# Attention scores on the TensorE array: whole array with zero-padded keys, or two halves of 64 rows

## The chip, the cores and the metric

The kernel runs on one core of a Trainium2 chip. The metric is device time in microseconds (us) of one execution.

## The reference

Cross-attention for x of 8 batches x 1024 queries x 640 features and a context of 64 tokens x 1024 features for each batch. Of the 64 tokens 56 are text and 8 are image tokens with a mask made from boxes. There are 20 heads of 32 features.

```
q = heads(x @ w_q)
k, v       = heads(text @ w_k), heads(text @ w_v)            # 56 keys
k_ip, v_ip = heads(ip @ w_k_ip), heads(ip @ w_v_ip)          # 8 keys
out = softmax(q k^T / sqrt(32)) v  +  softmax(q k_ip^T / sqrt(32) + mask) v_ip
out = merge_heads(out) @ w_out + b_out + x
```

Everything is float32. The kernel keeps its precision by splitting each operand of a product into a high part, rounded to float32r, and a low part, the rest; a product is the sum of three matmuls, high x high, high x low, low x high (`three`, L103).

## The kernel before

**Data layout.** x, q and the output have features on the 128 partitions, in KD = 5 tiles of 128 features, that is four heads each (HPT = 4). Queries go in groups of GQ = 512, two groups a batch, NG = 16 groups in all; a group has GT = 4 query tiles of 128.

**Setup (to about 92 us).** Weights are loaded and split; keys and values of the context are computed for all batches and go through k_scratch and v_scratch in HBM; the first q is computed.

**Keys.** k_raw holds the keys of one batch, a tile m of four heads by KEYS = 64 keys. A score matmul contracts over all 128 features of a tile, four heads at once, so the keys are laid out in blocks: k_hi and k_lo are [128, 5, 4, 64], and head j's keys stand only in its own 32 partitions and its own block j (`k_head`, L138); all else is zero, set once by two memsets (L279). The moving operand of one score matmul is one m of it, 4 x 64 = 256 columns, of which each row of the array has 64 that aren't zero. ScalarE writes the high parts (`k_hi_part`, four activations a batch), VectorE the low ones (`k_lo_part`).

**Scores.** The stationary operand is qT_hi or qT_lo, 128 features x 128 queries. `score_unit` (L841) fills one PSUM bank of 512 columns with two (query tile t, feature tile m) blocks of 256 scores, three matmuls each; a group has UNITS = 10 such units, on banks 0 to 3 in turn. ScalarE copies each bank to prob (`copy_scores`, L649) in SBUF, where a query tile has 20 heads x 64 keys = 1280 columns. From the fifth unit on, TensorE waits for the copy of the unit four before.

**The order of a group** is written out by hand for each engine; engines meet at semaphores alone. TensorE (`group`, L896): 10 score units; the 5 output tiles of the group before (75 matmuls of 512 columns); the first 2 of the 5 q tiles of the next group (30 of 75); then transposes of the probabilities by pairs of heads (`p_transpose`, L859), the products with v (`pv_pair`, L873) and the remaining 45 q matmuls interleaved. ScalarE: the score copies, with oT_hi of the group before after the second; exponentials; residual; copies of transposed probabilities and of results. GpSimd: adding the mask to the last 8 keys of each head when the tile's copies are done (`add_mask`, which waits for `units_for_tile`), in the order tiles 0, 1, 2, then subtracting the maximum from the tiles, the mask of tile 3 after tile 0, and then multiplying by the inverse sums (`normalise`). VectorE: maxima, sums, inverses, low parts, adding.

The transposes of a group can start only when GpSimd's `normalise` is done. Between the scores and the transposes TensorE has the output tiles and the q tiles.

Of the kernel before, what the change touches and what calls it, by code (L numbers as in the profile page):

```python
# [27 lines left out]
P = 128  # L28
# [11 lines left out]
def attention_kernel(nc, xT_dram, textT, ipT, bbox, w_q, w_k, w_v, w_k_ip, w_v_ip, w_out, b_out, grid_x, grid_y, outT):  # L40
# [14 lines left out]
    UNITS = GT * SW // 512  # L55
    HALF = D // 2
# [10 lines left out]
    with whole:  # L67
# [16 lines left out]
        k_hi, k_lo = sb("k_hi", [P, KD, HPT, KEYS], F32R), sb("k_lo", [P, KD, HPT, KEYS], F32R)  # L84
# [53 lines left out]
        def k_head(t, j):  # L138
            return t[j * DH:(j + 1) * DH, :, j, :]

        def k_hi_part(act, b):
            act.wait_ge(k_raw_loaded, 16 * (b + 1))
            for j in range(HPT):
                nc.scalar.activation(k_head(k_hi, j), k_raw[j * DH:(j + 1) * DH, :, :], ACT.Copy).then_inc(k_hi_built, 1)

        def k_lo_part(dve, b):
            for j in range(HPT):
                dve.wait_ge(k_hi_built, HPT * b + j + 1)
                nc.vector.tensor_tensor(k_head(k_lo, j), k_raw[j * DH:(j + 1) * DH, :, :], k_head(k_hi, j).bitcast(F32), ALU.subtract).then_inc(k_built, 1)
# [6 lines left out]
        with setup:  # L156
# [73 lines left out]
            with nc.Block() as block:  # L230
# [42 lines left out]
                @block.gpsimd  # L273
                def _(pool):
                    nc.gpsimd.memset(ident[:], 0.0).then_inc(ident_zeroed, 1)
                    pool.wait_ge(ident_zeroed, 1)
                    nc.gpsimd.affine_select(out=ident[:], in_=ident[:], compare_op=ALU.not_equal, fill=1.0, base=0,
                                            pattern=[[-1, P]], channel_multiplier=1).then_inc(ident_made, 1)
                    for buf in (k_hi, k_lo):  # L279
                        nc.gpsimd.memset(buf[:].rearrange("p m j k -> p (m j k)").bitcast(F32), 0.0).then_inc(k_zeroed, 1)  # L280
                    for c in range(1, len(chunks), 2):
                        hi, lo = split_dst(c)
                        pool.wait_ge(w_hi_done, c + 1)
                        nc.gpsimd.tensor_tensor(lo, w_raw[:, c % LOADS, :], hi.bitcast(F32), ALU.subtract).then_inc(w_lo_done[1], 1)

                @block.scalar
                def _(act):
# [42 lines left out]
                    for m in range(KD):  # L330
# [3 lines left out]
                        if m == KD - 3:  # L334
                            act.wait_ge(k_zeroed, 2)
                            k_hi_part(act, 0)
# [173 lines left out]
        def units_for_tile(t):  # L510

            return -(-(t + 1) * SW // 512)

        def tile(t):
            return prob[:, t * SW:(t + 1) * SW].rearrange("p (h k) -> p h k", k=KEYS)

# [43 lines left out]
        with nc.Block() as block:  # L560
# [87 lines left out]
            def _(act):  # L648
                def copy_scores(g, u):  # L649
                    act.wait_ge(score_ready, UNITS * g + u + 1)  # L650
                    nc.scalar.activation(prob[:, u * 512:(u + 1) * 512], s_bank[u % 4][:], ACT.Copy).then_inc(score_copied, 1)  # L651
# [188 lines left out]
            def _(pe):  # L840
                def score_unit(g, n, b, new_batch):  # L841
                    if n < 2:
                        wait(pe, score_copied, UNITS * g)
                    elif n < 4:
                        wait(pe, pT_lo_done, PAIRS * g)
                    else:
                        pe.wait_ge(score_copied, UNITS * g + n - 3)
                    if n == 0 and new_batch:
                        pe.wait_ge(k_built, HPT * (b + 1))
                    for half in range(2):  # L850
                        t, m = divmod(2 * n + half, KD)
                        if t == 0:
                            pe.wait_ge(q_lo_done, KD * g + m + 1)
                        q_cols = slice(t * P, (t + 1) * P)
                        keys = [k[:, m, :, :].rearrange("p j k -> p (j k)") for k in (k_hi, k_lo)]
                        ins = three(s_bank[n % 4][:, half * CW:(half + 1) * CW], qT_hi[:, m, q_cols], qT_lo[:, m, q_cols], *keys, True, True)
                    ins.then_inc(score_ready, 1)
# [38 lines left out]
                def group(g, b, new_batch, before, more, shared=0):  # L896
                    for n in range(UNITS):
                        score_unit(g, n, b, new_batch)
# [69 lines left out]
```

## Time and profile before

| | us |
|---|---|
| median of 2 runs | 929.83 (929.28 to 930.37) |
| span of the profiled execution | 927.5 |
| median less that span | 2.3 |
| TensorE matmul busy | 894.0 (96%) |
| VectorE busy | 732.2 (79%) |
| ScalarE busy | 605.7 (65%) |
| GpSimd busy | 520.5 (56%) |

The profile is of one execution. Its span goes from the first to the last instruction; the time of the run that was profiled isn't given beside it, so it is compared with the median. Recorded matmuls overlap, as each lasts until its results are written: how dense they are is told by the distance between starts. "PEld" rows are the loads of the stationary operand that each matmul brings with it. In the rows, "k_hi,qT_hi" means moving and stationary operand of a matmul; the three kinds of a product stand under the lines L104, L105 and L106 of `three`, whoever calls it. float32r operands are shown as f32.

### The profile page before, as it was taken

The page shows a single profiled execution, that of the slowest core. Times are in us where ns is not written, and L with a number is a line of the kernel's source. Part 1 is how long each engine was busy: PE and PEld are TensorE (multiplying, and loading weights), DVE is VectorE, ACT ScalarE, POOL GpSimd, SP SyncE. Part 2 cuts the span into 40 slices and gives each one's busy share as a digit, 9 for nine tenths or more (in the row PEclk, how much of TensorE's full clock was granted, in tenths as well). Part 3 has the DMA queues.
Part 4 walks back from the last instruction along what each step waited for, and adds up shares of the span by engine and source line. Part 5 has one row for each costly group of instructions (what it writes and reads, how often), then busy time and mean ns, then how long its engine had stood idle before and what let it go on. Part 6 is the DMA issues. An engine that isn't in the chain of part 4 may idle for free.

```text
span 927.5 us, 13827 instructions
## 1 busy us (share of the span) xinstructions
PE 894.0 (96%) x4685; PEld 749.3 (81%) x4685; DVE 732.2 (79%) x999; ACT 605.7 (65%) x982; POOL 520.5 (56%) x422
## 2 busy tenths in 40 slices
PE   7999869999999999999999999999999999999978
PEld 7977748888878788888888788888888887888856
DVE  6484888888787969787887879787887879697872
ACT  5464767585848577675858586775768485866751
POOL 3372638465573929374664839283755739292731
PEclk9999999999999999999999999999999999999989
DMA  8684020303030210303030301203030302010001
GB/s 264 222 275 162 22 71 1 121 1 128 1 121 1 72 55 4 116 0 127 0 120 0 121 6 38 83 0 127 0 120 0 127 0 91 22 47 12 35 23 57
DMA packets 34151, 64.79 MB, mean 70 GB/s; under 512 B 4428, under 2 KB 6604, under 8 KB 33996
## 3 DMA queue, kind: packets, MB, share of 16 engines
q1 hardware_dynamic: 32812, 61.82, 20.2%
q10 hardware_dynamic: 1312, 2.62, 0.9%
q8 instruction: 16, 0.26, 0.1%
q14 instruction: 11, 0.09, 0.0%
HBM read 40.84 MB, written 23.59 MB: 69 GB/s over the span
## 4 chain that ended last, share of the span: by engine, by line
PE 58%; DVE 18%; POOL 6%; issue 5%; ACT 2%; DVEq 0%; POOLq 0%
PE bank L104 15%; PE bank L106 14%; PE bank L105 14%; PE bank L870 7%; DVE total L764 5%; DVE xT_lo L118 5%; PE bank L879 4%; PE bank L880 4%; POOL prob L551 3%; DVE res L773 3%; POOL prob L606 2%; ACT prob L651 1%; DVE o_raw L753 1%; DVE top L758 1%; DVE pT_lo L746 1%
## 5 line engine op out<-in xcount | busy, mean ns | idle before, releaser
L618 POOL TENSOR_TENSOR oT_lo<-o_raw,oT_hi 128x512 fp32r<-128x512 f32 x80 | 103.3, 1292 | 266.2 <-ACT oT_hi L671 266.2
L551 POOL TENSOR_TENSOR prob<-prob,top 128x1120 f32<-128x1120 f32 x124 | 174.4, 1435 | 0.0
L557 POOL TENSOR_TENSOR prob<-prob,inv 128x1120 f32<-128x1120 f32 x124 | 164.4, 1361 | 6.9 <-DVE inv L766 6.9
L104 PE MATMUL bank<-xT_hi,wq_hi 128*128 128x512 f32 x400 | 163.0, 408 | 2.6 <-DVE qT_lo L136 2.6
L104 PE MATMUL bank<-oT_hi,wo_hi 128*128 128x512 f32 x400 | 159.8, 400 | 3.1 <-DVE res L773 2.3
L105 PE MATMUL bank<-oT_lo,wo_hi 128*128 128x512 f32 x400 | 158.0, 395 | 0.0
L106 PE MATMUL bank<-oT_hi,wo_lo 128*128 128x512 f32 x400 | 157.9, 395 | 0.0
L106 PE MATMUL bank<-xT_hi,wq_lo 128*128 128x512 f32 x400 | 157.0, 393 | 0.0
L105 PE MATMUL bank<-xT_lo,wq_hi 128*128 128x512 f32 x400 | 155.9, 390 | 0.0
L753 DVE TENSOR_TENSOR o_raw<-bank,pv_part 64x512 f32<-64x512 f32 x160 | 110.2, 689 | 49.1 <-ACT pv_part L667 45.1
L758 DVE TENSOR_REDUCE top<-prob 128x20 f32<-128x1120 f32 (+1 forms) x128 | 98.7, 814 | 43.6 <-POOL prob L606 43.3
L658 ACT ACTIVATE prob<-prob 128x1280 f32<-128x1280 f32 x64 | 81.5, 1275 | 77.9 <-POOL prob L551 76.7
L667 ACT ACTIVATE pv_part<-bank 64x512 f32<-64x512 f32 x160 | 94.8, 593 | 40.3 <-PE bank L880 37.1
L132 ACT ACTIVATE qT_hi<-bank 128x512 fp32r<-128x512 f32 x80 | 47.3, 591 | 103.6 <-PE bank L106 101.0
L746 DVE TENSOR_TENSOR pT_lo<-bank,pT_hi 128x512 fp32r<-128x512 f32 x160 | 108.0, 683 | 3.5 <-ACT pT_hi L662 1.5
L662 ACT ACTIVATE pT_hi<-bank 128x512 fp32r<-128x512 f32 x160 | 94.1, 599 | 12.8 <-PE bank L870 9.7
L118 DVE TENSOR_TENSOR xT_lo<-xin,xT_hi 128x512 fp32r<-128x512 f32 x80 | 101.2, 1282 | 0.0
L651 ACT ACTIVATE prob<-bank 128x512 f32<-128x512 f32 x160 | 92.6, 598 | 11.3
L870 PEld LDWEIGHTS bank<-ident,prob 128*128 128x128 f32 x640 | 79.8, 142 | 23.2 <-POOL prob L557 3.6
L870 PE MATMUL bank<-ident,prob 128*128 128x128 f32 x640 | 95.1, 275 | 3.1 <-POOL prob L557 3.1
L764 DVE TENSOR_REDUCE total<-prob 128x20 f32<-128x1120 f32 (+1 forms) x128 | 98.0, 805 | 0.0
L104 PEld LDWEIGHTS bank<-oT_hi,wo_hi 128*128 128x128 f32 x400 | 75.0, 188 | 27.0 <-DVE res L773 9.0
(88 smaller groups left out, 1754.3 us busy)
## 6 DMA issues: line engine op xcount, KB each, us to landing
outT<-res SPq DMA_DIRECT2D x80, 256.0 KB, 6.7
xin<-in_xT SPq DMA_DIRECT2D x14, 1280.0 KB, 6.7
w_raw<-in_L_xattn_w_v SPq DMA_DIRECT2D x8, 320.0 KB, 5.3
w_raw<-in_L_xattn_w_k SPq DMA_DIRECT2D x8, 320.0 KB, 3.6
w_raw<-in_L_xattn_w_v_ip SPq DMA_DIRECT2D x8, 320.0 KB, 3.8
w_raw<-in_L_xattn_w_k_ip SPq DMA_DIRECT2D x8, 320.0 KB, 3.7
xin<-in_xT ACTq DMA_DIRECT2D x2, 1280.0 KB, 8.0
v_raw<-v_scratch SPq DMA_DIRECT2D x16, 160.0 KB, 4.2
```

The costliest lines, as they stand in the source:

```text
L104: nc.tensor.matmul(dst, a_hi, b_hi, start=first, stop=False)
L105: nc.tensor.matmul(dst, a_hi, b_lo, start=False, stop=False)
L106: return nc.tensor.matmul(dst, a_lo, b_hi, start=False, stop=last)
L118: nc.vector.tensor_tensor(x_tile(xT_lo, k), xin[:, u, k, :], x_tile(xT_hi, k).bitcast(F32), ALU.subtract).then_inc(xT_lo_done, 1)
L551: ins = eng.tensor_tensor(s, s, top[:, t, n, :].unsqueeze(2).broadcast_to([P, HEADS, k1 - k0]), ALU.subtract)
L557: ins = eng.tensor_tensor(s, s, inv[:, t, n, :].unsqueeze(2).broadcast_to([P, HEADS, k1 - k0]), ALU.mult)
L618: nc.gpsimd.tensor_tensor(oT_lo[:, m, :], o_raw[:, m % 2, :], oT_hi[:, m, :].bitcast(F32), ALU.subtract).then_inc(oT_lo_done, 1)
L746: nc.vector.tensor_tensor(pT_lo[:, p % 2, :], t_bank[p % 2][:], pT_hi[:, p % 2, :].bitcast(F32), ALU.subtract).then_inc(pT_lo_done, 1)
L753: nc.vector.tensor_tensor(o_raw[own, m % 2, :], v_bank[p % 2][own, :], pv_part[own, :], ALU.add).then_inc(pv_added, 1)
L758: ins = nc.vector.tensor_reduce(top[:, t, n, :], tile(t)[:, :, k0:k1], AX.X, ALU.max)
L764: nc.vector.tensor_reduce(total[:, t, span, :], tile(t)[:, :, k0:k1], AX.X, ALU.add).then_inc(sum_done, 1)
L870: ins = nc.tensor.transpose(t_bank[p % 2][:, t * P:(t + 1) * P], src, ident[:])
```

## The change

The array is used in two halves of 64 rows, r = 0 and r = 1. Each half contracts over two heads, 64 features, and its moving operand has only these two heads' keys: PW = 2 x 64 = 128 columns. The results of the two halves are different columns of the scores, and they go to different banks: a pair of banks (n, n + 1) is filled by RUN = 4 steps (t, m); bank n gets the first two heads of the four steps, bank n + 1 the others. So each step has 3 x 2 matmuls of 64 rows and 128 columns, the halves in turn. Both banks of a pair are ready after the last step, and TensorE waits before each pair for both banks. The copies on ScalarE write four runs of 128 columns. The zero-padded keys are one buffer, k_parts, with high and low parts and two head blocks for each. units_for_tile gives 4, 6, 8, 10 where it gave 3, 5, 8, 10.

```diff
+    PW = 2 * KEYS
+    RUN = 512 // PW
...
-        k_hi, k_lo = sb("k_hi", [P, KD, HPT, KEYS], F32R), sb("k_lo", [P, KD, HPT, KEYS], F32R)
+        k_parts = sb("k_parts", [P, KD, 2, 2, KEYS], F32R)
...
-        def k_head(t, j):
-            return t[j * DH:(j + 1) * DH, :, j, :]
+        def k_head(part, j):
+            return k_parts[j * DH:(j + 1) * DH, :, part, j % 2, :]
...
-                    for buf in (k_hi, k_lo):
-                        nc.gpsimd.memset(buf[:].rearrange("p m j k -> p (m j k)").bitcast(F32), 0.0).then_inc(k_zeroed, 1)
+                    nc.gpsimd.memset(k_parts[:].rearrange("p m s j k -> p (m s j k)").bitcast(F32), 0.0).then_inc(k_zeroed, 1)
...
         def units_for_tile(t):
-            return -(-(t + 1) * SW // 512)
+            return 2 * -(-(t + 1) * KD // RUN)
...
+        def score_dst(u):
+            blocks = prob[:, u // 2 * RUN * CW:(u // 2 + 1) * RUN * CW].rearrange("p (n r c) -> p r n c", r=2, c=PW)
+            return blocks[:, u % 2, :, :]
...
-                    nc.scalar.activation(prob[:, u * 512:(u + 1) * 512], s_bank[u % 4][:], ACT.Copy).then_inc(score_copied, 1)
+                    nc.scalar.activation(score_dst(u), s_bank[u % 4][:].rearrange("p (n c) -> p n c", n=RUN), ACT.Copy).then_inc(score_copied, 1)
...
-                def score_unit(g, n, b, new_batch):
-                    if n < 2:
+                def score_units(g, u, b, new_batch):
+                    n = 2 * u
+                    if u == 0:
                         wait(pe, score_copied, UNITS * g)
-                    elif n < 4:
+                    elif u == 1:
                         wait(pe, pT_lo_done, PAIRS * g)
                     else:
-                        pe.wait_ge(score_copied, UNITS * g + n - 3)
-                    if n == 0 and new_batch:
+                        pe.wait_ge(score_copied, UNITS * g + n - 2)
+                    if u == 0 and new_batch:
                         pe.wait_ge(k_built, HPT * (b + 1))
-                    for half in range(2):
-                        t, m = divmod(2 * n + half, KD)
+                    for i in range(RUN):
+                        t, m = divmod(RUN * u + i, KD)
                         if t == 0:
                             pe.wait_ge(q_lo_done, KD * g + m + 1)
-                        q_cols = slice(t * P, (t + 1) * P)
-                        keys = [k[:, m, :, :].rearrange("p j k -> p (j k)") for k in (k_hi, k_lo)]
-                        ins = three(s_bank[n % 4][:, half * CW:(half + 1) * CW], qT_hi[:, m, q_cols], qT_lo[:, m, q_cols], *keys, True, True)
-                    ins.then_inc(score_ready, 1)
+                        q_cols, dst = slice(t * P, (t + 1) * P), slice(i * PW, (i + 1) * PW)
+                        for q_part, k_part in ((qT_hi, 0), (qT_hi, 1), (qT_lo, 0)):
+                            for r in range(2):
+                                rows = slice(r * HP, (r + 1) * HP)
+                                ins = nc.tensor.matmul(s_bank[(n + r) % 4][:, dst], q_part[rows, m, q_cols], k_parts[rows, m, k_part, :, :].rearrange("p j k -> p (j k)"),
+                                                       start=q_part is qT_hi and k_part == 0, stop=q_part is qT_lo)
+                                if i == RUN - 1 and q_part is qT_lo:
+                                    ins.then_inc(score_ready, 1)
```

## Rows read from the trace of the kernel before

**Rows 1.** The page: busy us, share and instructions; granted TensorE clock in tenths, 40 slices.

```profile
PE 894.0 (96%) x4685; PEld 749.3 (81%) x4685; DVE 732.2 (79%) x999; ACT 605.7 (65%) x982; POOL 520.5 (56%) x422
...
PEclk9999999999999999999999999999999999999989
```

**Rows 2.** The waits of TensorE: us in total, times, longest us.

```profile
PE bank L879 <- DVE pT_lo L746: 11.3, 17, 2.0
PE bank L104 <- DVE ipT_parts L380: 6.0, 1, 6.0
PE bank L870 <- POOL prob L557: 3.1, 2, 2.6
PE bank L104 <- DVE qT_lo L136: 2.6, 1, 2.6
...
PE bank L104 <- DVE res L773: 2.3, 13, 0.2
```

**Rows 3.** Windows: a score stage and a whole group; us, then busy us (instructions), clock.

```profile
499.45:506.75 7.30, 7.30 (x61) 7.30 (x61) 4.98 (x7) 6.69 (x12) 3.33 (x5) 1.00 0.00 0
...
499.45:550.90 51.45, 51.27 (x271) 43.08 (x271) 42.04 (x58) 34.85 (x57) 30.53 (x26) 1.00 0.17 57
```

**Rows 4.** Groups by line and shape: count, busy us, mean ns, idle before.

```profile
L104 PE MATMUL bank<-k_hi,qT_hi 128*128 128x256 f32 x320 | 91.2, 285 | 1.6 <-PEq L230 1.1 <-ACT prob L651 0.5
...
L651 ACT ACTIVATE prob<-bank 128x512 f32<-128x512 f32 x160 | 92.6, 598 | 11.3
```

**Rows 5.** Timeline of TensorE, start and end of that score stage: start us, us.

```profile
499.47 0.37 PE L104 MATMUL bank<-k_hi,qT_hi 128*128 128x256 f32 x1
499.68 0.28 PE L105 MATMUL bank<-k_lo,qT_hi 128*128 128x256 f32 x1
499.80 0.28 PE L106 MATMUL bank<-k_hi,qT_lo 128*128 128x256 f32 x1
...
499.45 0.19 PEld L104 LDWEIGHTS bank<-k_hi,qT_hi 128*128 128x128 f32 x1 [0.26 <-issue]
499.56 0.19 PEld L105 LDWEIGHTS bank<-k_lo,qT_hi 128*128 128x128 f32 x1
499.68 0.19 PEld L106 LDWEIGHTS bank<-k_hi,qT_lo 128*128 128x128 f32 x1
499.80 0.19 PEld L104 LDWEIGHTS bank<-k_hi,qT_hi 128*128 128x128 f32 x1
...
506.63 0.28 PE L106 MATMUL bank<-k_hi,qT_lo 128*128 128x256 f32 x1
506.75 0.40 PE L104 MATMUL bank<-oT_hi,wo_hi 128*128 128x512 f32 x1
...
506.63 0.19 PEld L104 LDWEIGHTS bank<-oT_hi,wo_hi 128*128 128x128 f32 x1
```

**Rows 6.** Timeline of TensorE in the setup, matmuls of 320 columns, first and last of six.

```profile
12.80 0.31 PE L104 MATMUL bank<-qT_hi,ctxT_hi 128*112 128x320 f32 x1
...
13.53 0.31 PE L106 MATMUL bank<-qT_hi,ctxT_lo 128*112 128x320 f32 x1
```

**Rows 7.** Weight loads by shape, windows 14 to 30 and 40 to 60 us: mean ns.

```profile
L106 PEld LDWEIGHTS bank<-qT_hi,ctxT_lo 128*112 128x112 f32 x37 | 6.5, 174 | 0.0
...
L104 PEld LDWEIGHTS bank<-ctxT_hi,qT_hi 128*128 128x128 f32 x21 | 3.9, 187 | 3.8 <-POOL qT_lo L284 3.5
```

**Rows 8.** Timeline and source line: the five transposes of k_ip; min/median/max ns.

```profile
74.02 0.39 PEld L468 LDWEIGHTS bank<-ident,k_ip 64*128 64x128 f32 x5 [0.31 <-issue]
...
L468 PEld LDWEIGHTS bank<-ident,k_ip x5: 134/140/140, 74.0 to 74.3; 64*128 64x128 f32 x5
```

**Rows 9.** Timeline of TensorE: the next group's first eight transposes and what follows.

```profile
531.53 1.03 PE L870 MATMUL bank<-ident,prob 128*128 128x128 f32 x8
532.32 0.48 PE L104 MATMUL bank<-xT_hi,wq_hi 128*128 128x512 f32 x1
```

**Rows 10.** Timeline of ScalarE over that score stage.

```profile
499.36 1.21 ACT L667 ACTIVATE pv_part<-bank 64x512 f32<-64x512 f32 x2
500.59 1.20 ACT L651 ACTIVATE prob<-bank 128x512 f32<-128x512 f32 x2
501.69 0.62 ACT L671 ACTIVATE oT_hi<-o_raw 128x512 fp32r<-128x512 f32 x1
502.21 5.34 ACT L651 ACTIVATE prob<-bank 128x512 f32<-128x512 f32 x8
```

**Rows 11.** Timeline of GpSimd: the last normalisations of that group.

```profile
518.88 10.54 POOL L557 TENSOR_TENSOR prob<-prob,inv 128x1120 f32<-128x1120 f32 x8
```

**Rows 12.** Source line of the key memsets: min/median/max ns, first and last start us.

```profile
L280 POOL MEMSET k_hi<- x1: 1164/1164/1164, 1.4 to 1.4; 128x1280 f32 x1
L280 POOL MEMSET k_lo<- x1: 1164/1164/1164, 2.5 to 2.5; 128x1280 f32 x1
```

More of the change, by code:

```diff
@@ L143, in k_hi_part @@
             for j in range(HPT):
-                nc.scalar.activation(k_head(k_hi, j), k_raw[j * DH:(j + 1) * DH, :, :], ACT.Copy).then_inc(k_hi_built, 1)
+                nc.scalar.activation(k_head(0, j), k_raw[j * DH:(j + 1) * DH, :, :], ACT.Copy).then_inc(k_hi_built, 1)
         def k_lo_part(dve, b):
@@ L148, in k_lo_part @@
                 dve.wait_ge(k_hi_built, HPT * b + j + 1)
-                nc.vector.tensor_tensor(k_head(k_lo, j), k_raw[j * DH:(j + 1) * DH, :, :], k_head(k_hi, j).bitcast(F32), ALU.subtract).then_inc(k_built, 1)
+                nc.vector.tensor_tensor(k_head(1, j), k_raw[j * DH:(j + 1) * DH, :, :], k_head(0, j).bitcast(F32), ALU.subtract).then_inc(k_built, 1)
         def load_k(sp, b):
@@ L334, in _ @@
                         if m == KD - 3:
-                            act.wait_ge(k_zeroed, 2)
+                            act.wait_ge(k_zeroed, 1)
                             k_hi_part(act, 0)
@@ L896, in group @@
                 def group(g, b, new_batch, before, more, shared=0):
-                    for n in range(UNITS):
-                        score_unit(g, n, b, new_batch)
+                    for u in range(UNITS // 2):
+                        score_units(g, u, b, new_batch)
                     if before:
```

## The prediction

> **What bounds the kernel now.** I read the page's busy times first. TensorE has 894.0 of 927.5 us, its clock was granted at nine or ten tenths throughout, and no other engine passes 80% [rows 1]. Busy matmul time can deceive, so next the waits of TensorE: the largest sum is 11.3 us, behind VectorE's pT_lo, and all the others together come to some 19 us [rows 2]. Then one whole group of 512 queries in the windows: 51.45 us, of which TensorE records 51.27 as busy [rows 3]. Sixteen such groups run one after another, 823 of the 927.5 us. So in the steady state the end is set by how closely TensorE's instructions follow each other, and what a score stage costs TensorE, the whole kernel pays sixteen times. The stage itself lasts 7.30 us and holds 60 matmuls of 256 columns; recorded durations (283 ns) overlap, and it is the spacing that counts [rows 3, 4, 5].
>
> **What a score matmul costs now.** In the timeline each starts 0.12 us after the one before, and the load of the next weights starts at the very moment the current matmul starts [rows 5]. Is the matmul or the load the limit? At 320 columns six starts lie 0.146 us apart [rows 6]. At 2.4 GHz, one column each cycle, 320 columns take 133 ns and 256 take 107: both leave 13 ns. So the streaming is the limit and the load is hidden, but only just. Where a load is not hidden, at the first score matmul after a pause, the second load follows 0.11 us after the first [rows 5]. The shape table supports this price: loads of 112 columns are recorded at 174 ns, loads of 128 at 187 or 188, so 16 columns are worth 14 ns, and 128 of them 110 [rows 7]. These are rows of 128 partitions; a load of the float32r kind with 64 partitions is nowhere in the trace.
>
> The Trainium skill, "TensorE: Matmul & The Clock Gate", section "LDWEIGHTS (loading the stationary operand)", gives columns / 1.2 ns, 107 ns for 128 columns, whatever the number of rows; the rows above agree with its size, and that 64 rows cost the same is shown by none.
>
> **The change, part by part.**
>
> Columns. The zeros of the other two heads of a tile are no longer streamed: a (tile, m, part) step moves 128 columns in each half and not 256 in the whole array. If both halves stream at once, this is 53 + 13 = 66 ns for a step instead of 120.
>
> Instructions and loads. 60 matmuls become 120, and each still brings its own load of 128 weight columns: 120 loads instead of 60. Removed: streaming. Doubled: everything paid per instruction. Three prices for a pair of halves follow. (a) Streaming alone, 66 ns. (b) The load of the next pair can't hide behind 53 ns of streaming: 110 to 120 ns if the two halves load side by side, 220 to 240 if one after the other. (c) The closest spacing of two matmuls anywhere in the trace is that of the five small transposes of k_ip, 64 rows and 64 columns: their five loads span 0.39 us, the last of them 0.14, so 0.0625 us apart [rows 8]. If that is the pace of issue, a pair can't take less than 125 ns. The transposes of 128 columns are no tighter than 0.11 us each (eight from 531.53 to about 532.4) [rows 9]. I take 125 ns: the halves use different rows, different partitions of SBUF and different banks, and it is the price from the row that is nearest in size, with 64 rows. The ends for the range are 66 and 240. So 60 pairs take 7.5 us, and with the 0.10 us of the exposed first load 7.6, against 7.30 now: **+0.3 us a group**.
>
> Score copies. They stay 160 ScalarE copies of 128x512, 598 ns each [rows 4]; the destination becomes four runs of 128 elements, for which I count nothing; a run of 128 floats is long, and if it did cost 50 ns each, 10 copies would be 0.5 us a group, of which the next point shows about half on the path. But two banks now come ready together, after 24 matmuls (1.5 us) and not after 6 (0.7 us). ScalarE today is free 1.12 us after the stage begins (pv_part ends at 500.57), copies from 500.59, has oT_hi after the second copy, and ends the ten at 507.55 [rows 10]. After the change it starts at about +1.75 us. The pair of banks for the fourth step is free when 4 copies are done: 1.75 + 2.4 + 0.42 for oT_hi = 4.6, plus some 0.1 of signalling, against 4.6 us at which TensorE would be there: **+0.1 to 0.25 us**, take 0.2. For the fifth step 6 copies are needed, at 5.8, and TensorE arrives at 6.3: no wait. Behind a waiting TensorE is only its own stream; ScalarE, on the other hand, ends its copies 0.6 us later.
>
> Leaving the halves. Today the first wo_hi load is issued at 506.63, during the last score matmul, and hidden [rows 5]. After it the array goes back from half to full rows. If that load must wait for the halves, 0.11 us are exposed, and with the end of the last matmul (283 less 120 ns) up to 0.28. Entering is less: the stage already begins with an exposed load. I take **+0.15 us**.
>
> The Trainium skill, "TensorEngine Tiling (Array Packing)", section "Key Properties", says that changing the tiling mode drains TensorE; by it the upper end of 0.28 us would hold at both ends of the stage, and the sum would be some 6 us longer. No row here has such a change of mode.
>
> Masks and probabilities. GpSimd's mask for tile 0 now waits for 4 copies, not 3, and for tile 1 for 6, not 5; for tiles 2 and 3 for 8 and 10 as before. GpSimd's long chain (subtract, normalise) starts in order behind the mask of tile 2, so with copy 8, some 0.5 us later. It ends at 529.42 today, the transposes that need it start at 531.53 [rows 9, 11]: 2.1 us of slack, and they move later themselves. Nothing is added. If this slack were gone, a delay of the copies would be paid in full, 0.6 x 16 = 10 us.
>
> Key buffers. k_hi and k_lo (2 x 1280 words a partition) become k_parts with half of that; one memset of 1.16 us in place of two at 1.4 us into the kernel [rows 12], used 85 us later: nothing. The splits into high and low parts have the same 32x320 shapes, same strides in kind: nothing. No DMA is changed.
>
> **The sum.** 0.3 + 0.2 + 0.15 = 0.65 to 0.7 us a group, 16 groups: +11 us on the span of 927.5, so 938.5; the median of the runs (929.83) stands 2.3 us above that span: **941 us**.
>
> **Rivals.**
>
> 1. *The two halves load one after the other.* Place: each of the 120 loads; price: 0.11 us each, 13.2 and 0.1 us for the stage against 7.3, +6.0 and 0.15 for leaving, x 16 = +98: **1028 us** (1023 to 1047 for 107 to 120 ns). It decides as soon as a pair needs more than about 137 ns (8.3 us for the stage, +19 us, 2%). For it: today every load begins only when the matmul before it has begun, as if one could be ahead at a time [rows 5], and if that order is kept across the halves, 64 rows buy nothing. Against it: that same timing is explained as well by the one spare set of weights, which is free only when the matmul starts, and the halves have each their own. The k_ip loads (64 rows, 0.0625 us apart) prove only that small float32 loads are short. 30%.
> 2. *The halves overlap in part*: loads side by side, but one matmul streams after the other with something lost in each turn, or every bank change stalls: 150 to 200 ns a pair, 9.1 to 12.1 us for the stage, +31 to +79: **961 to 1009 us**. Nothing speaks for one value. 10%.
> 3. *The pair really takes the time of its streaming*, 66 ns, because a load of 64 rows is short and the pace of issue isn't 62 ns. Then ScalarE's copies set the stage: six copies and oT_hi must be done before the last step, 1.14 + 6 x 0.6 + 0.43 + 0.1 = 5.3 us, and 0.8 for it: 6.1 against 7.3, less 0.15 for leaving, so -1.0 x 16: **914 us**, just inside 2%. Against it: 110 ns for a load of this kind in two readings [rows 5, 7]. 8%.
>
> The Trainium skill, "TensorEngine Tiling (Array Packing)", sections "Theoretical Speedup" and "PSUM Bottleneck", promises up to 2x for a contraction of at most 64 rows and warns that the emptying of PSUM may then be the bottleneck; that is this third case.
>
> That the change doesn't do what it says (both halves stream in turn, loads hidden) would be 2 x 66 = 132 ns a pair, +0.7 us a group instead of +0.3: 947 us, and lies in the forecast's own range.
>
> **How the numbers follow.** Forecast 941 with its neighbours (pairs of 110 to 135 ns, leaving 0 to 0.3 us), 926 to 952: 52%. With the rivals at 30, 10 and 8% that is everything. Two per cent, about what a measurement of this kernel can tell from no change, is 911.2 to 948.4. Faster: the better half of rival 3, 3%. Within: 48% of the forecast's 52, nearly 5% of rival 3, 2% of the rest: 55%. Slower: 42%. The range reaches from 914 up to 1034, leaving out 4% below and the upper third of rival 1 and stray cases above.
>
> **What will show it.** In the timeline of the score stage, the starts of two neighbouring matmuls of different halves and of two of the same half: 0.12 to 0.13 us for the latter and a stage of about 8 us if I am right, 0.21 to 0.24 and a stage near 13 us under rival 1, under 0.1 us and a stage near 6 under rival 3. The load rows: whether two loads of different halves start together. A wait of TensorE for a score copy before the fourth step of a group, and none for it under rival 1. The first wo_hi load: during the last score matmul, or after it. The prediction is wrong if the halves load in turn, and above all if ScalarE's copies with their four runs are longer than 0.65 us.

## The result: 943.35 us, 1.5% slower, and the profile after

The changed kernel takes **943.35 us** (median of two runs, 938.98 and 947.71) against 929.83 before; the ratio is 1.0148 [1.0123, 1.0172]. Run again beside other kernels it took 939.75 us, ratio 1.0102 [1.0085, 1.0119]. Its profiled execution spans 937.2 us, 9.7 more than the one before. That is the forecast's size (941). But of its terms one has the wrong sign, one that was put at nothing is as large as the whole loss of a group, and one was not in it.

The page of the changed kernel: busy times; the granted clock of TensorE in 40 slices; two groups of instructions.

```profile
PE 899.8 (96%) x5645; PEld 749.1 (80%) x5645; DVE 723.4 (77%) x999; ACT 599.4 (64%) x982; POOL 518.1 (55%) x421
...
PEclk9999799999999999999999999999999999999999
...
L865 PE MATMUL bank<-k_parts,qT_hi 64*128 64x128 f32 x1280 | 114.9, 281 | 1.9 <-PEq L232 1.0
...
L657 ACT ACTIVATE prob<-bank 128x512 f32<-128x512 f32 x160 | 86.8, 597 | 26.2 <-PE bank L865 26.0
```

TensorE has 960 instructions more (60 x 16) and is busy for only 6 us more. The copies are as long as before, 597 ns against 598 [rows 4]; their idle time before them has grown from 11.3 to 26.2 us, nearly all of it spent waiting for score banks. The fifth slice of the clock is new.

The waits of TensorE in the changed kernel (us in total, times, longest).

```profile
PE bank L106 <- DVE res L779: 9.1, 15, 0.6
...
PE bank L865 <- ACT prob L657: 0.9, 1, 0.9
```

One row has moved: the wait for VectorE's res, 2.3 us in 13 waits [rows 2], is 9.1 in 15. That is the wait before an output tile. The wait for a score copy stands here once in the whole run, so what it costs in every group is read from starts, below.

Windows of the changed kernel: the ninth group's score stage and the whole group (us, then busy us and instructions of TensorE, its loads, VectorE, ScalarE, GpSimd; granted clock; DMA).

```profile
506.43:513.47 7.04, 7.04 (x121) 6.89 (x120) 3.83 (x6) 5.75 (x11) 2.77 (x4) 1.00 0.00 0
506.43:558.30 51.87, 51.24 (x333) 42.60 (x332) 41.62 (x58) 34.47 (x57) 30.64 (x26) 1.00 0.17 57
```

**The stage is shorter** by 0.26 us [rows 3], **and the group longer** by 0.42. Before, stages alternate between 7.28 and 7.20 us, groups between about 51.46 and 51.37, so the mean change is -0.20 and +0.45. In the table further down, the first two rows and 0.09 us of the leaving add up to the stage's change, all four rows to the group's.

The timeline of TensorE and of its loads, changed kernel, at the start and the end of that stage (start us, us). The timeline merges neighbours that are alike; the second row is what starts in the 10 ns from 506.43.

```profile
506.11 0.39 PE L891 MATMUL bank<-pT_lo,v_parts 128*128 128x512 f32 x1
506.43 0.33 PE L865 MATMUL bank<-k_parts,qT_hi 64*128 64x128 f32 x2
...
506.71 0.27 PE L865 MATMUL bank<-k_parts,qT_lo 64*128 64x128 f32 x2
506.82 0.39 PE L865 MATMUL bank<-k_parts,qT_hi 64*128 64x128 f32 x4
507.04 0.27 PE L865 MATMUL bank<-k_parts,qT_lo 64*128 64x128 f32 x2
...
513.27 0.27 PE L865 MATMUL bank<-k_parts,qT_lo 64*128 64x128 f32 x2
513.47 0.50 PE L106 MATMUL bank<-oT_hi,wo_hi 128*128 128x512 f32 x1
513.81 0.39 PE L107 MATMUL bank<-oT_lo,wo_hi 128*128 128x512 f32 x1
...
506.43 0.19 PEld L865 LDWEIGHTS bank<-k_parts,qT_hi 64*128 64x128 f32 x2 [0.35 <-issue]
...
513.47 0.19 PEld L106 LDWEIGHTS bank<-oT_hi,wo_hi 128*128 128x128 f32 x1
```

Both loads of a pair and both matmuls start within the same 10 ns. Three pairs (four matmuls on qT_hi, two on qT_lo) take 0.33 us, 506.71 to 507.04, so a pair takes 0.111. The prediction's sign for being right was a stage of about 8 us; this one, 7.04, is neither that nor the 13 or 6 of its rivals. The first wo_hi load now starts at 513.47, after the last score matmul and not with it [rows 5].

The timelines of ScalarE and GpSimd of the changed kernel: the copies, and the mask of tile 2.

```profile
506.25 1.21 ACT L673 ACTIVATE pv_part<-bank 64x512 f32<-64x512 f32 x2
508.02 1.09 ACT L657 ACTIVATE prob<-bank 128x512 f32<-128x512 f32 x2 [0.56 <-PE bank L865]
...
509.51 1.09 ACT L657 ACTIVATE prob<-bank 128x512 f32<-128x512 f32 x2
...
512.24 1.09 ACT L657 ACTIVATE prob<-bank 128x512 f32<-128x512 f32 x2 [0.40 <-PE bank L865]
...
513.51 0.52 POOL L612 TENSOR_TENSOR prob<-prob,mask 128x160 f32<-128x160 f32 x1 [0.47 <-ACT prob L657]
```

Copies come in twos, each two behind a pair of banks; the fourth two, from 512.24, end at 513.33, 6.90 us into the stage. Where that delay is paid is seen ten microseconds later. First the kernel before, then the changed one: TensorE before the fifth output tile, with the VectorE steps that release it and the mask of tile 2 at the head of their chain.

```profile
506.30 0.53 POOL L606 TENSOR_TENSOR prob<-prob,mask 128x160 f32<-128x160 f32 x1 [1.04 <-ACT prob L651]
...
518.52 1.53 DVE L764 TENSOR_REDUCE total<-prob 128x20 f32<-128x1120 f32 x2
520.41 0.63 DVE L773 TENSOR_TENSOR res<-bank,res 128x512 f32<-128x512 f32 x1
...
520.52 0.39 PE L106 MATMUL bank<-oT_hi,wo_lo 128*128 128x512 f32 x1
521.09 0.50 PE L104 MATMUL bank<-oT_hi,wo_hi 128*128 128x512 f32 x1 [0.18 <-DVE res L773]
```

```profile
525.80 1.53 DVE L770 TENSOR_REDUCE total<-prob 128x20 f32<-128x1120 f32 x2
527.69 0.63 DVE L779 TENSOR_TENSOR res<-bank,res 128x512 f32<-128x512 f32 x1
...
527.34 0.40 PE L108 MATMUL bank<-oT_hi,wo_lo 128*128 128x512 f32 x1
528.37 0.50 PE L106 MATMUL bank<-oT_hi,wo_hi 128*128 128x512 f32 x1 [0.63 <-DVE res L779]
```

Matmuls here are 0.23 us apart. Before, the fifth tile came 0.57 after its predecessor, now 1.03. The fifth tile needs a bank that VectorE's `output` of the third tile empties, and that addition stands in VectorE's order behind `sums` of query tile 1, which waits for the exponentials, which wait for GpSimd's subtraction, which stands behind the mask of tile 2, which waits for copy 8. From that mask's start to the late matmul it is 14.8 us before and 14.9 after: the chain was without slack already, and what delays copy 8 delays TensorE. The loss of 0.34 us was there before the change in nearly every group, and the last row of [rows 2], 13 waits, is where it stood.

### The profile page after: what moved, and what is told of

The parts are those of the page before. It is cut to its first block, busy times and chain, and to the rows that moved or that the text cites. A ratio compares the mean times of both kernels' runs of the same rounds, so it can differ in the third digit from the quotient of the medians.

```text
span 937.2 us, 15707 instructions
## 1 busy us (share of the span) xinstructions
PE 899.8 (96%) x5645; PEld 749.1 (80%) x5645; DVE 723.4 (77%) x999; ACT 599.4 (64%) x982; POOL 518.1 (55%) x421
## 4 chain that ended last, share of the span: by engine, by line
PE 59%; DVE 17%; issue 7%; POOL 4%; ACT 3%; DVEq 0%; POOLq 0%; ACTq 0%
PE bank L106 12%; PE bank L108 11%; PE bank L107 11%; PE bank L865 10%; PE bank L881 7%; DVE total L770 5%; DVE xT_lo L120 5%; PE bank L890 4%; PE bank L891 4%; DVE res L779 3%; POOL prob L557 2%; POOL prob L612 2%; ACT prob L657 1%; DVE o_raw L759 1%; DVE top L764 1%
## 5 line engine op out<-in xcount | busy, mean ns | idle before, releaser
L865 PE MATMUL bank<-k_parts,qT_hi 64*128 64x128 f32 x1280 | 114.9, 281 | 1.9 <-PEq L232 1.0
L865 PEld LDWEIGHTS bank<-k_parts,qT_hi 64*128 64x128 f32 x1280 | 100.0, 193 | 9.1 <-issue 6.9
L657 ACT ACTIVATE prob<-bank 128x512 f32<-128x512 f32 x160 | 86.8, 597 | 26.2 <-PE bank L865 26.0
```

The costliest lines, as they stand in the source:

```text
L657: nc.scalar.activation(score_dst(u), s_bank[u % 4][:].rearrange("p (n c) -> p n c", n=RUN), ACT.Copy).then_inc(score_copied, 1)
L865: ins = nc.tensor.matmul(s_bank[(n + r) % 4][:, dst], q_part[rows, m, q_cols], k_parts[rows, m, k_part, :, :].rearrange("p j k -> p (j k)" ...
```

## The experiments

Each kernel is the one before or the changed one with the edit shown. "Steady group" is a group's length, score stage to score stage, for the third to the fourteenth group: 51.37 to 51.54 us before, 51.84 to 51.92 in the changed kernel.

### The price of a load

**b_whole_128**: the kernel before with every score matmul cut in two of 128 columns, all 128 rows.

```diff
-                        keys = [k[:, m, :, :] ... for k in (k_hi, k_lo)]
-                        ins = three(s_bank[n % 4][:, half * CW:(half + 1) * CW], ...)
+                        for r in range(2):
+                            keys = [k[:, m, 2 * r:2 * r + 2, :] ... for k in (k_hi, k_lo)]
+                            c0 = half * CW + r * CW // 2
+                            ins = three(s_bank[n % 4][:, c0:c0 + CW // 2], ...)
```

> The kernel before, but each score matmul of 256 columns is cut into two of 128 columns, both over the whole array (128 rows), so 120 matmuls and 120 loads in place of 60, nothing side by side. Theory (a load of 128 float32r columns takes 0.111 us and is the price of a matmul too short to hide it, and only loads of different halves run together): 0.111 us a matmul, score stage 13.3 us, and some 5.7 us a group more in the total, about 1015 to 1025 us. Rival (the 0.111 us for a pair of matmuls is the pace of issue, 0.055 us for each): stage 6.7 to 7.2 us, time 926 to 935 us.

Measured: 1040.3 us, ratio 1.1181 [1.1116, 1.1246]. Timeline of TensorE in this kernel, start of a stage:

```profile
552.27 0.31 PE L104 MATMUL bank<-k_hi,qT_hi 128*128 128x128 f32 x1
552.42 0.27 PE L105 MATMUL bank<-k_lo,qT_hi 128*128 128x128 f32 x1
552.53 0.27 PE L106 MATMUL bank<-k_hi,qT_lo 128*128 128x128 f32 x1
552.64 0.28 PE L104 MATMUL bank<-k_hi,qT_hi 128*128 128x128 f32 x1
```

0.111 us a matmul, the stage 13.35 to 13.45 us. A matmul of the whole height now costs the 0.111 us that a pair of halves costs. The same 0.11 us lies between the first two loads of a stage when the matmuls have 256 columns [rows 5], so it is the load and not the matmul, and what the halves buy is that two loads go side by side. The time is above the expectation because the stage isn't all: the steady group is 58.2 to 58.3 us, and TensorE's wait for res is there too (10.0 us in 14 waits). The second of its two runs also had a lower mean clock, 0.984 against 0.995, and took 10 us longer.

The Trainium skill, "TensorE: Matmul & The Clock Gate", section "LDWEIGHTS (loading the stationary operand)", has columns / 1.2 ns whatever the number of rows, an estimate of 107 ns for 128 columns; the 0.111 us for 128 and for 64 rows agree.

**a_rows_apart**: the changed kernel, but within a pair of banks all twelve matmuls of one half before the twelve of the other.

```diff
-                    for i in range(RUN):
+                    for r, i in [(r, i) for r in range(2) for i in range(RUN)]:
...
-                            for r in range(2):
```

> The changed kernel with the same 120 matmuls of 64 rows and 128 columns, but in each pair of banks the 12 of the first half all come before the 12 of the second. Theory (loads of one half wait for each other, only the two halves load side by side): 0.111 us a matmul, stage about 13.3 us, 1015 to 1025 us. Rival (pace of issue, or a 64-row load that simply takes half the time): 0.055 us a matmul, stage as in the changed kernel, 7.1 us, 935 to 945 us.

Measured: 1077.44 us, ratio 1.158 [1.1524, 1.1636]. Timeline of TensorE at full clock, then the window of a later stage, in this kernel:

```profile
391.52 0.39 PE L865 MATMUL bank<-k_parts,qT_hi 64*128 64x128 f32 x2
391.75 0.27 PE L865 MATMUL bank<-k_parts,qT_lo 64*128 64x128 f32 x1
391.75 0.49 PE L865 MATMUL bank<-k_parts,qT_hi 64*128 64x128 f32 x4
...
270.00:285.80 15.80, 15.80 (x121) 15.66 (x121) 6.53 (x9) 6.79 (x12) 5.45 (x7) 0.61 0.01 2
```

Matmuls of one half alone follow each other at 0.111 us, the same as a pair (two on qT_hi, then one on qT_lo 0.23 us later). The halves run at once only where matmuls of both stand close together in the program. Two surprises. At 391.75 the first of the second half starts while three of the first half, written ahead of it, have yet to start. And the granted clock falls in every score stage, to half, 1.2 GHz, for a part of it (0.61 on average in this one; stages of 13.3 to 16.5 us), which no profile with alternating halves shows in the stage of any group but the first. So its 147 us hold, besides the halves in turn, an overlap that was not intended and a low clock, and are no clean price.

**a_rows_by_three**: the halves alternate by three matmuls and not by one.

```diff
-                        for q_part, k_part in (...):
-                            for r in range(2):
+                        for r in range(2):
+                            for q_part, k_part in (...):
```

> The changed kernel, but in each step the three matmuls of the first half come before the three of the second. It shows how far ahead of matmuls that still wait a load of the other half can be taken. If only past one matmul: two of six loads overlap with one of the other half, four load times a step, 0.44 us, stage 8.9 us, time about 965 us. If past three or more: 0.335 us a step as in the changed kernel, stage 7.1 us, 943 us. If past none: 0.67 us a step, stage 13.3 us, 1020 us.

Measured: 939.66 us, ratio 1.0099 [1.0078, 1.012], a stage of 7.05 us: the changed kernel's time. Its timeline at the start of a stage:

```profile
402.82 0.44 PE L865 MATMUL bank<-k_parts,qT_hi 64*128 64x128 f32 x4
403.10 0.28 PE L865 MATMUL bank<-k_parts,qT_lo 64*128 64x128 f32 x2
```

In the program the order is hi, hi, lo of one half and then of the other; in the trace all four on qT_hi start before either on qT_lo. A matmul of the other half goes past those written before it. With three of one half in a row the order costs nothing; with twelve it does.

### Where the group gets longer

**b_pair_ready**: the kernel before, whole rows and 256 columns, but two banks become ready together, at the end of each 12 matmuls. The loop over 10 units becomes one over 5 pairs; for such a pair:

```diff
-                        pe.wait_ge(score_copied, UNITS * g + n - 3)
+                        pe.wait_ge(score_copied, UNITS * g + n - 2)
...
+                    order = [(i, 0, part) for i in range(2) for part in range(3)] + [(i, 1, part) for part in range(3) for i in range(2)]
+                    for i, half, part in order:
```

> The kernel before with its 60 whole-array matmuls of 256 columns, but ordered so that two banks are finished 0.12 us apart, after 12 matmuls, and TensorE waits for both banks of a pair: one part of the change, its readiness in pairs, without the halves. Theory (what the change costs in the steady groups comes in by the eighth score copy, which starts GpSimd's chain, and is paid at TensorE's wait before the fifth output tile): score stage still 7.2 us, the copies some 0.2 to 0.35 us later, the stretch from the first output matmul to the first transpose longer by about as much (24.8 to 25.1 us), 51.65 to 51.85 us a group, 933 to 936 us, clock of the first group unchanged. Rival (the added 0.4 us a group is the price of going in and out of the halves): nothing changes, 930 us.

Measured: 936.39 us, ratio 1.0065 [1.0044, 1.0085]. Its TensorE and ScalarE, by timeline, and the wait row:

```profile
422.55 0.39 PE L106 MATMUL bank<-oT_hi,wo_lo 128*128 128x512 f32 x1
423.50 0.50 PE L104 MATMUL bank<-oT_hi,wo_hi 128*128 128x512 f32 x1 [0.56 <-DVE res L773]
...
511.26 1.09 ACT L651 ACTIVATE prob<-bank 128x512 f32<-128x512 f32 x2 [0.35 <-PE bank L858]
...
PE bank L104 <- DVE res L773: 8.1, 15, 0.6
```

No halves, the stage 7.2 to 7.29 us as before, and yet the steady group is 51.73 to 51.97, about what was expected: **handing banks over two at a time is enough for the longer wait at the fifth output tile**, and for nearly all of the steady loss.

**b_mask** and **a_mask**: an attempt to make slack elsewhere. GpSimd starts the chain with tile 0 before it adds the mask of tile 2, except in the first and the last group, and VectorE makes its first two xT_lo parts one tile earlier.

```diff
                     add_mask(g, 1)
-                    add_mask(g, 2)
+                    if shared:
+                        add_mask(g, 2)
                     for t, count in tiles:
                         sub_max(g, t, count)
                         if t == 0:
+                            if not shared:
+                                add_mask(g, 2)
                             add_mask(g, 3)
...
-                        if before and t == 2:
+                        if before and t == (2 if shared else 1):
                             split_x(0, 2)
```

> The kernel before, with GpSimd subtracting the maximum of tile 0 before it adds the masks of tiles 2 and 3 (not in the first and the last group), and VectorE's first two xT_lo parts after the maxima of tile 1 instead of tile 2. GpSimd's chain then starts behind the copy of unit 5 and not of unit 8. Theory: TensorE's wait of 0.45 us (with the exposed load) before the fifth output tile goes, 51.0 us a group, 13 or 14 groups: 923 to 926 us, ratio 0.993 to 0.996. Rival (the chain is held elsewhere, VectorE's order above all): no change or up to 1% slower, because the output of tile 0 comes later behind the maxima of tile 3.

> The changed kernel with the same reordering on GpSimd and VectorE. Theory (the steady loss of the change was that chain alone; halves as such cost nothing net): its wait of 0.9 us before the fifth output tile goes, 51.0 us a group as in the same reordering of the kernel before, total 926 to 931 us, with 2 to 4 us more than that one from the half clock in the first group. Rival (going in and out of the halves costs TensorE 0.4 us a group): 0.4 us a group more than the reordered kernel before, some 6 us, plus the first group: 932 to 936 us.

Measured: b_mask 946.13 us, 1.0192 [1.0167, 1.0217], and a_mask 958.52, 1.0322 [1.0291, 1.0352]. Both miss, theory and rival. The VectorE timeline of b_mask:

```profile
412.38 1.64 DVE L118 TENSOR_TENSOR xT_lo<-xin,xT_hi 128x512 fp32r<-128x512 f32 x2 [1.26 <-ACT xT_hi L114]
```

VectorE, in its fixed order, now stands 1.26 us for an xT_hi of ScalarE, and its output tiles come later: TensorE's wait for res is 17.5 us in 18 waits in b_mask and 21.8 in 29 in a_mask. The edit moved more than the chain, so it tells nothing about the chain's slack.

**b_output2**, **a_output2**: VectorE's order alone. The output addition of the third tile goes ahead of `sums` of query tile 1, of which it needs nothing.

```diff
+                        if before and n == 1:
+                            output(g - 1, 1 - u, n + 1)
                         sums(g, t, n)
...
-                        if before:
+                        if before and n != 1:
                             output(g - 1, 1 - u, n + 1)
```

> The kernel before, with VectorE adding output tile 2 of the group before (which frees the bank of the fifth output tile) ahead of the sums of tile 1 instead of after them; nothing else. Theory (TensorE's wait before the fifth output tile is for this one instruction, which stands behind sums that wait for GpSimd's chain): the wait of 0.45 us with its exposed load goes, 51.0 us a group, 14 groups: 923 to 925 us, ratio 0.993 to 0.995. Rival (the chain is late by as much further on, at the q tiles or at the transposes): 929 to 931 us.

> The changed kernel with the same move of output tile 2 on VectorE. Theory: its wait of 0.9 us goes; score stage with way in and out 0.1 us more than nothing, so about 51.0 us a group as in the same move in the kernel before, and 2 to 4 us for the half clock in the first group: 926 to 930 us, ratio 0.996 to 1.000; level or faster than the kernel before. Rival (the halves cost 0.4 us a group on TensorE itself): 51.4 us a group, 934 us.

Measured: the kernel before with it 925.71 us, ratio **0.9962 [0.9949, 0.9975]**, faster than both kernels. Its steady groups take 50.98 to 51.38 us, and the list of waits has res with 0.2 us in one. The changed kernel with it takes 935.94, ratio 1.0073 [1.0043, 1.0104], steady groups 51.45 to 51.53: the theory misses, the rival's numbers come out. Its TensorE and VectorE show why:

```profile
479.41 0.39 PE L108 MATMUL bank<-oT_hi,wo_lo 128*128 128x512 f32 x1
480.05 0.49 PE L106 MATMUL bank<-xT_hi,wq_hi 128*128 128x512 f32 x1 [0.24 <-DVE res L779]
...
477.40 1.53 DVE L770 TENSOR_REDUCE total<-prob 128x20 f32<-128x1120 f32 x2
479.29 0.63 DVE L779 TENSOR_TENSOR res<-bank,res 128x512 f32<-128x512 f32 x1
```

The fifth tile no longer waits, and the first q tile, one place on, waits 0.4 us for the fourth addition, which still stands behind the sums. So the rival's numbers came out for another reason than the one that it gave.

The kernel before with it isn't quite free of this either. In five of its twelve steady groups, those of 51.26 us and more, the first q tile comes 0.47 us after the matmul before it and not 0.23, again just behind the fourth addition (574.36 to 574.99), and leaves its load exposed:

```profile
574.65 0.39 PE L106 MATMUL bank<-oT_hi,wo_lo 128*128 128x512 f32 x1
575.12 0.49 PE L104 MATMUL bank<-xT_hi,wq_hi 128*128 128x512 f32 x1
```

The other seven take 50.98 to 51.11.

**a_output23**: the fourth addition is moved the same way (`n in (1, 2)` in place of `n == 1`).

> The changed kernel with VectorE adding output tiles 2 and 3 of the group before each ahead of the sums that they stood behind (tile 2 alone moved TensorE's wait to the first q matmul, where output tile 3 frees the bank). Theory (halves cost TensorE itself nothing net: 0.09 us more at the entry, 0.1 at the exit, 0.15 to 0.25 less in the stage; the rest is VectorE and GpSimd being late): that wait of 0.5 us goes, 50.9 to 51.1 us a group, as in the whole-array kernel with output tile 2 moved (51.05 to 51.3), and with the half clock of the first group 928 to 931 us. Rival (0.4 us a group is lost in the halves whatever is reordered): 51.4 to 51.5 us a group, 934 to 937 us.

Measured in 12 runs: 929.5 us, ratio 0.9994 [0.9983, 1.0004], no difference from the kernel before. Windows of a score stage and of a group, and the wait row, in this kernel:

```profile
500.45:507.50 7.05, 7.05 (x122) 6.90 (x121) 3.81 (x6) 5.73 (x11) 2.76 (x4) 1.00 0.00 0
500.45:551.44 50.99, 50.99 (x333) 42.68 (x332) 41.31 (x58) 34.45 (x57) 31.02 (x26) 1.00 0.17 58
...
PE bank L106 <- DVE res L779: 0.6, 1, 0.6
```

TensorE has no pause in the whole group. It is 0.88 us shorter than in the changed kernel: the 0.80 of the wait and 0.1 of the load that it left exposed. Where neither waits, halves and whole rows take the same time for a group within 0.1 us: 50.99 to 51.01 here, 50.98 to 51.11 in b_output2. Whole rows with both additions moved were not run, and the best time on record stays that of whole rows, 925.71 us. The profiled spans of the two, 927.9 and 925.9, differ by the first group (2.3 us longer here, see below), the setup (1.3) and the last group (1.7, not looked into), less 3.2 in the groups between.

### The first group, and the spread of runs

**a_again** is the changed kernel unedited. **m_g0_whole** has the first group's scores in whole rows from k_hi and k_lo, and halves of the same buffers from the second group on (`score_units` if g > 0, else `score_unit`).

> The changed kernel once more, for an interval on its ratio and a second profile of the clock. Theory: the steady groups are the same as in the first profile (51.86 us each, 0.41 more than before), and the score stage of the first group again runs partly at half clock, so that its 7.98 us become about 12; ratio 1.010 to 1.016. Rival: the fall of the clock in the first group was chance; then that stage lasts 7.8 to 8.2 us, the span is near 933.5 and the ratio near 1.006.

> The changed kernel's halves in all groups but the first; the first group's scores are made over the whole array as in the kernel before (keys in the layout of before, which holds the same 128 columns for each half). Theory (the half clock in the first score stage comes from the matmuls of 64 rows): that stage runs at full clock and lasts 7.9 to 8.0 us, the total is 2 to 4 us less than the changed kernel's, 936 to 937 us; the later groups stay at 51.87 us. Rival (the clock falls there by chance or for the pause before it, whatever the matmuls): the stage is 9.6 us or more as before, 940 us.

Measured: a_again 939.75 us, 1.0102 [1.0085, 1.0119], span 936.8, and m_g0_whole 936.51, 1.0092 [1.0062, 1.0123], span 934.4. Windows of the changed kernel and of m_g0_whole in the first group's score stage, which begins at 92.8 and 93.0 us:

```profile
98.00:105.00 7.00, 7.00 (x65) 6.88 (x66) 4.08 (x5) 2.31 (x5) 2.46 (x4) 0.50 0.00 0
```

```profile
98.00:105.00 7.00, 7.00 (x44) 6.32 (x44) 5.56 (x7) 4.90 (x8) 5.21 (x7) 1.00 0.00 0
```

In the changed kernel the clock is at 1.2 GHz for 13.7 us from 95.3 on, pairs are 0.21 us apart, and the stage takes 11.92 us; in whole rows in the same place it stays at 2.4 GHz and takes 7.98, as before the change. a_again has the low clock for 6.8 us and a stage of 9.65, less than the 12 that were expected. So it goes in every profile: the seven kernels with halves in the first group have 6.8 to 17.1 us of low clock that begin in this stage, the seven with whole rows have none there. The span of m_g0_whole is 2.8 us below that of the changed kernel; the ratios of a_again and m_g0_whole overlap, so in the timed runs the gain isn't proved.

Whole rows are not immune elsewhere. Every profile but that of the kernel before has a low stretch of 3.4 us that begins somewhere from 113 to 141 us. In b_output2 it falls into the score stage of the second group, which follows a stretch in which TensorE was busy for 2.35 of 3.9 us; that stage takes 8.68 us, and 7.18 in the kernel before. b_mask has the same. The windows are of b_output2:

```profile
136.00:139.90 3.90, 2.35 (x11) 1.51 (x11) 2.70 (x5) 3.38 (x6) 1.79 (x2) 1.00 0.00 0
140.20:143.60 3.40, 3.40 (x18) 3.40 (x18) 1.04 (x2) 2.20 (x4) 0.32 (x1) 0.50 0.00 0
```

**m_output2** joins m_g0_whole and the edit of a_output2.

> Halves in all groups but the first, which has its scores over the whole array, and the same move of output tile 2 on VectorE. Theory: as a_output2, without the half clock of the first group: 924 to 927 us, level with b_output2 within 2 us; then the halves are worth nothing either way. If the halves gain after all (stage 7.15 us against 7.2 to 7.3), it is b_output2 less 1 us.

Measured: 938.95 us (932.02 to 940.02, five runs), 1.01 [1.0086, 1.0115]; the theory misses. The profiled execution spans 930.2, with steady groups of 51.46 to 51.65, near those of a_output2. The other four spans are 6 to 8 us longer, and each run's mean granted clock is on record: 0.994 in the profiled one, 0.985 to 0.987 in those four. From these means it is 13 to 17 us more at half clock. At half the clock TensorE does half the work (0.21 us a pair against 0.111), so by an estimate this costs 6.5 to 8.5 us, about the difference. Those four runs were not profiled, so where in the kernel the low clock falls stays open; the first score stage has whole rows here.

The other kernels go the same way: the changed kernel's two runs span 937.2 at 0.989 and 945.9 at 0.984; a_output2 spans 930.7 at 0.991 and 941.5 at 0.980; m_g0_whole 933.8 to 935.1 in three runs at 0.995 or 0.996 and 940.8 at 0.987; b_whole_128 1033.6 at 0.995 and 1043.4 at 0.984. Kernels whose score matmuls have 256 columns throughout stay at 0.994 to 0.998 in every run. As b_whole_128 has whole rows, the 64 rows are not the only way to a lower clock; what it shares with the halves are matmuls of 128 columns, each with its own load. Not all spread is clock: b_mask has 950.0 at 0.996.

## Why the prediction was right in size and wrong in its terms

By a steady group, in us:

| step | predicted | measured | from |
|---|---|---|---|
| 60 pairs in place of 60 matmuls | +0.3 | -0.5 | pair 0.111, not 0.125 |
| wait before the fourth pair of banks | +0.2 | +0.2 | 0.1, and 0.1 of loads left exposed |
| entering and leaving | +0.15 | +0.3 | below |
| GpSimd's chain | 0 | +0.45 | fifth output tile |
| sum | +0.65 to 0.7 | +0.45 | windows |

**Step (c), the price of a pair, is the mis-sized term.** The 62.5 ns between the k_ip transposes [rows 8] were taken as a pace of issue; two matmuls start in 10 ns here, so there is no such pace. Those transposes are plain float32 with 64 moving columns; why their loads of 64 rows and 128 columns come closer than the 0.111 of these isn't shown. The limit is the load: 0.111 us, what [rows 5] had for a load of 128 rows, the lower end of the prediction's own (b). Against 0.12 a matmul before, it is 60 x -0.009 = -0.5.

**Entering and leaving.** The first score matmul comes 0.32 us after the last product with v, 0.23 before; after the last pair the wo_hi load starts 0.09 us late and is itself exposed, 0.11 (the next matmul comes 0.34 and not 0.23 later). Together 0.3, twice the term, and the first load exposed on the way out is as foretold.

The Trainium skill, "TensorEngine Tiling (Array Packing)", section "Key Properties", has the array drain at a change of mode. The trace doesn't contradict it: all that is lost is 0.1 us on the way in and 0.2 on the way out, the exposed load included, not the prediction's 0.28 at each.

**The copies** that matter end later by 0.34 us, not 0.6: from the start of the last product with v to the mask behind the eighth copy it is 7.40 us, 7.06 before. With the 0.07 by which the rest of the chain is longer, the late matmul comes 0.41 later, while TensorE itself is at its place as early as before (21.23 us after that product, 21.28 before). The wait before the fourth pair of banks (the prediction's fourth step) is there: its first two matmuls come 0.21 after their predecessors and not 0.11, just behind the fourth copy, and its load, like that of the third, leaves 0.05 exposed.

**"Nothing is added" is the step that failed.** The slack of 2.1 us was measured where the chain ends, at the transposes, past an engine order that is tied to it earlier. b_pair_ready shows the price alone, the edits of the output additions take it away, and in a_output23 what is left of the sum is nothing. The prediction priced a delay without slack at 0.6 x 16 = 10 us; it was 0.45 x 14 = 6.3, and it was there.

**What was not in it:** the clock in the first group, 3.9 us of the profiled 9.7 (50.63 against 46.69). The prediction read the clock as nine or ten tenths throughout; one slice near the end stands at 8 [rows 1], and nothing in the trace of before pointed at the first group. With 6.3 for the groups between and -0.45 for the last, which was not looked into, the 9.7 is complete. So +9.7 against +11 is a sum of errors that cancel: the time was met by luck.

**The rivals.** One load after the other (30%) is out: loads of a pair start together, and the stages of b_whole_128, 13.35 to 13.45 us, show the price if they didn't. A pair at its streaming time (8%) is out: pairs come 0.111 us apart, not 0.066. A loss in each turn (10%) is out in steady groups. The expectation that four runs of 128 might slow the copies is out: 597 ns.

## What to carry to other kernels

Cutting a matmul into row halves with half the columns halves the streaming only. Each half still loads 128 weight columns, and at 0.111 us a pair against 0.12 for 256 columns nothing is left to win once the ends are paid. When an edit delays a chain, take its slack at the first wait of the bounding engine on anything in the order of the engines that the chain passes, even if it is 0.2 us in thirteen places, and not where the chain ends. And when buffers begin to come ready in twos, treat that as a change of its own: here it cost more than the halves did, and putting two additions ahead of the sums gave it back.

## What the runs showed of the hardware that was not expected

- Matmuls of 64 rows in the other half start ahead of matmuls written before them: in a_rows_by_three ahead of two, in a_rows_apart at 391.75 ahead of three.
- TensorE's granted clock fell to 1.2 GHz while it was recorded busy. With alternating halves this was in the first group's score stage, in every profile; in the changed kernel it was busy for 5.8 of the 6.8 us before that stage and 2.47 of the stage's first 2.5. With one half at a time it was in every stage (mean 0.89 over a_rows_apart). Seven profiles with whole rows keep 2.4 GHz in that first stage, though two of them lose it for 3.4 us in the second group's. Why the alternating halves keep the clock from the second group on in the profiled executions was not tried.
- At either level the load sets the pace: 0.111 us for a pair with 128 float32r weight columns at 2.4 GHz, 0.21 at 1.2.
